# A second expert bias in TensorE's sums: a two-part F32R product in place of two VectorE operations per tile

## What is computed

```python
x = x + gnn(layernorm(x), adj, ...)              # 32 graphs, hidden width 512
xin = layernorm(x)                               # input of the experts
xn = layernorm_affine(xin, gamma, beta)
logits = xn @ Wr + br                            # 8 experts
top_vals, top_idx = jax.lax.top_k(logits, 2)
w = jax.nn.softmax(top_vals)                     # weights of the two chosen experts
for e in range(8):
    h = gelu(xn @ W1[e] + b1[e])                 # 128 -> 256
    y_e = h @ W2[e] + b2[e]                      # 256 -> 128
    y = y + y_e * w_full[..., e, None]
x = x + y
```

## Time and profile before

| | us |
|---|---|
| median of 3 runs | 456.43 (456.37 to 456.51) |
| the profiled execution | 457.52 |
| its span, first to last instruction | 455.7 |
| TensorE matmul busy | 405.1 |
| TensorE weight load busy | 346.2 |
| VectorE busy | 306.7 |
| ScalarE busy | 278.8 |
| GpSimd busy | 247.0 |

### The profile page before, as it was taken

The page is one execution under the profiler, slowest core; times in us unless marked ns, Lnnn a source line. Parts: engine busy times, 40 slices in busy tenths (PEclk is TensorE's granted clock), DMA queues, the critical chain, the costliest instruction groups (busy, mean ns, idle before and its releaser), DMA issues.

```text
span 455.7 us, 11870 instructions
## 1 busy us (share of the span) xinstructions
PE 405.1 (89%) x2894; PEld 346.2 (76%) x2894; DVE 306.7 (67%) x1303; ACT 278.8 (61%) x645; POOL 247.0 (54%) x315
## 2 busy tenths in 40 slices
PE   0999999999999999999856675999899999999994
PEld 0457777767777777786746675998899899999994
DVE  4487677898887788867745374676566666655562
ACT  1167777777677778777737262666566666534451
POOL 1023347766667876775744536454555655555554
PEclk9999999999999999999996978899999999999998
DMA  6659762333323231011154224455544454333211
GB/s 190 198 169 353 267 195 98 102 108 93 118 79 109 84 117 39 35 49 39 48 156 121 70 63 127 114 151 138 141 136 132 109 139 115 101 104 108 84 36 36
DMA packets 40889, 53.24 MB, mean 117 GB/s; under 512 B 5811, under 2 KB 35635, under 8 KB 40182
## 3 DMA queue, kind: packets, MB, share of 16 engines
q1 hardware_dynamic: 33040, 32.95, 25.9%
q0 software_dynamic: 6096, 18.52, 11.9%
q10 hardware_dynamic: 1686, 1.01, 0.8%
HBM read 37.75 MB, written 22.31 MB: 132 GB/s over the span
## 4 chain that ended last, share of the span: by engine, by line
PE 57%; issue 10%; DVE 10%; DVEq 8%; another core or an unknown queue 5%; ACT 4%; POOL 2%; DMA 2%; ACTq 1%; POOLq 0%
PE banks L576 10%; PE banks L599 10%; PE banks L724 9%; PE banks L737 8%; PE banks L564 6%; PE banks L585 5%; PE banks L621 3%; DVEq L1434 2%; DVEq L1417 2%; PE banks L611 2%; DMA rms_bc<-rms_w 2%; DVE result L1442 2%; PE banks L706 1%; DVEq L1442 1%
## 5 line engine op out<-in xcount | busy, mean ns | idle before, releaser
L526 POOL DMA_INDIRECT out<-result,rows_in x92 | 89.5, 973 | 83.7 <-DVE result L1442 71.8
L737 PE MATMUL banks<-w_sb,hidden_e 128*128 (+1 forms) x736 | 102.2, 283 | 5.9 <-DVE result L1442 5.0
L737 PEld LDWEIGHTS banks<-w_sb,hidden_e 128*128 128x128 f32 x736 | 92.4, 196 | 9.5 <-issue 8.7
L877 ACT ACTIVATE hidden_e<-banks 128x512 f32<-128x512 f32 x92 | 54.9, 597 | 60.9 <-PE banks L724 35.8
L489 POOL DMA_INDIRECT rows_dram<-rows_out,row_of x64 | 66.5, 1039 | 24.8 <-issue 22.0
L599 PE MATMUL banks<-gw_sb,hidden_t 128*128 128x128 f32 x512 | 68.8, 277 | 0.0
L576 PE MATMUL banks<-gw_sb,agg 128*128 128x512 f32 x128 | 67.2, 611 | 0.8 <-ACT agg L812 0.8
L1428 DVE SCALAR_TENSOR_TENSOR acc<-banks,rows_in,acc 128x128 f32<-128x128 f32 x92 | 32.2, 350 | 48.8 <-PE banks L737 21.0
L599 PEld LDWEIGHTS banks<-gw_sb,hidden_t 128*128 128x128 f32 x512 | 63.5, 192 | 0.8
L797 ACT ACTIVATE hidden<-hidden,rrms 128x512 f32<-128x512 f32 x64 | 45.6, 714 | 18.1 <-POOL rrms L466 18.1
L990 DVE TENSOR_TENSOR hidden<-banks,rms_bc 128x512 f32<-128x512 f32 x64 | 43.8, 686 | 13.8 <-ACT hidden L789 13.8
(11 more groups left out here) (141 smaller groups left out, 707.9 us busy)
## 6 DMA issues: line engine op xcount, KB each, us to landing
rows_in<-rows_dram SPq DMA_DIRECT2D x92, 132.5 KB
adj<-adj_t SPq DMA_DIRECT2D x16, 512.0 KB, 3.7
x_tok<-x SPq DMA_DIRECT2D x16, 256.0 KB, 3.7
rows_dram<-idle_in POOLq DMA_DIRECT2D x1, 3710.0 KB
rows_dram<-idle_in SPq DMA_DIRECT2D x28, 132.5 KB
out<-result,rows_in POOLq DMA_INDIRECT x92
w_sb<-w SPq DMA_DIRECT2D x1, 1024.0 KB, 6.3
b_bc<-b SPq DMA_DIRECT2D x1, 1024.0 KB, 11.5
```

The costliest lines, as they stand in the source:

```text
L526: nc.gpsimd.indirect_dma_start(out=out, out_offset=bass.IndirectOffsetOnAxis(ap=rows_in[:, i % RING][:, IDX_AT:IDX_AT + 1].bitcast(U32), a ...
L737: last = pe.matmul(y_ps(i)[:, w], hidden_e[:, i % 4, w * HCE + c], w2_sb[:, bass.ds(at + c * D, D)], start=(c == 0), stop=(c == HCE - 1))
L877: nc.scalar.activation(hidden_e[:, i % 4], h_ps(i), ACT.Gelu).then_inc(gelu_done, 1)
```

## The change

The bias is no longer added by VectorE. For each of a tile's two experts TensorE begins the sum in PSUM with `bias_sel` times the expert's 128 columns of `b2_parts`, an F32R matmul, and the two matmuls of the second layer add to it. `b2_parts` (128 x 1024, zero but for row 0, the rounded bias, and row 32, the remainder) is made once on VectorE in steps 11 to 14, each of its four operations last in its step; the rounded copy in row 32 lies in `b1_bc`. L1417 and L1434 and their waits and semaphores are gone; the low product (L1428 before) now adds the residual values directly. TensorE waits for `b2_split` before its first tile.

```diff
+        b2_parts = sb("b2_parts", [P, E * D], F32R)
+        b2_high = b1_bc[:, 0:E * D].bitcast(F32R)
...
                     for w in range(2):
+                        bias_at = expert(words, i, D, w == 0)
+                        pe.matmul(y_ps(i)[:, w], bias_sel[:], b2_parts[:, bass.ds(bias_at, D)], start=True, stop=False)
                         at = expert(words, i, HE, w == 0)
                         for c in range(HCE):
                             last = pe.matmul(y_ps(i)[:, w], hidden_e[:, i % 4, w * HCE + c],
-                                             w2_sb[:, bass.ds(at + c * D, D)], start=(c == 0), stop=(c == HCE - 1))
+                                             w2_sb[:, bass.ds(at + c * D, D)], start=False, stop=(c == HCE - 1))
...
             pe.wait_ge(table_ready, 2)
+            pe.wait_ge(b2_split, 4)
...
+            def split_b2(k):
+                if k == 0:
+                    dve.wait_ge(folded, FOLDS)
+                    nc.vector.memset(b2_parts[:].bitcast(F32), 0.0).then_inc(b2_split, 1)
+                elif k == 1:
+                    dve.wait_ge(b2_split, 1)
+                    nc.vector.tensor_copy(b2_parts[0:1], b2_bc[0:1]).then_inc(b2_split, 1)
+                elif k == 2:
+                    nc.vector.tensor_copy(b2_high[32:33], b2_bc[32:33]).then_inc(b2_split, 1)
+                else:
+                    dve.wait_ge(b2_split, 3)
+                    nc.vector.tensor_tensor(b2_parts[32:33], b2_bc[32:33], b2_high[32:33].bitcast(F32), ALU.subtract
+                                            ).then_inc(b2_split, 1)
...
+                if s - FOLD_AT - FOLDS in range(4):
+                    split_b2(s - FOLD_AT - FOLDS)
...
             def tile_step(step):
-                if (i := tile_at(step, 0)) is not None:
-                    rows = rows_in[:, i % RING]
-                    if i < NT and i % PER_WORD == 0:
-                        words[i // PER_WORD % 2] = dve.value_load(word[0:1, i // PER_WORD:i // PER_WORD + 1],
-                                                                  min_val=0, max_val=2 ** 24 - 1)
-                    dve.wait_ge(rows_here[i % RING], 16 * (i // RING + 1))
-                    if i >= AHEAD:
-                        dve.wait_ge(result_ready, i - AHEAD + 1)
-                    nc.vector.scalar_tensor_tensor(acc[:, i % AHEAD], b2_bc[:, bass.ds(expert(words, i, D, True), D)],
-                                                   rows[:, bass.ds(expert(words, i, 1, True) + W_AT, 1)],
-                                                   rows[:, X2_AT:X2_AT + D], ALU.mult, ALU.add).then_inc(based, 1)
                 tail(step, 0)
...
-                    dve.wait_ge(base_done, j + 1)
                     dve.wait_ge(y_done, j + 1)
+                    if j >= AHEAD:
+                        dve.wait_ge(result_ready, j - AHEAD + 1)
                     nc.vector.scalar_tensor_tensor(acc[:, j % AHEAD], y_ps(j)[:, 0],
                                                    done[:, bass.ds(expert(done_words, j, 1, True) + W_AT, 1)],
-                                                   acc[:, j % AHEAD], ALU.mult, ALU.add).then_inc(low_added, 1)
+                                                   done[:, X2_AT:X2_AT + D], ALU.mult, ALU.add).then_inc(low_added, 1)
                 tail(step, 1)
-                if i is not None:
-                    dve.wait_ge(based, i + 1)
-                    nc.vector.scalar_tensor_tensor(acc[:, i % AHEAD], b2_bc[:, bass.ds(expert(words, i, D, False), D)],
-                                                   rows[:, bass.ds(expert(words, i, 1, False) + W_AT, 1)],
-                                                   acc[:, i % AHEAD], ALU.mult, ALU.add).then_inc(base_done, 1)
```

More of the change, by code:

```diff
@@ L277, in build @@
         folded = sem("folded")
+        b2_split = sem("b2_split")
         rank_consts = sem("rank_consts")
@@ L337, in build @@
         y_done = sem("y_done")
-        based = sem("based")
-        base_done = sem("base_done")
         low_added = sem("low_added")
@@ L1404, in tail @@
                     table_words(1, 2)
-            words = {}
             def tile_step(step):
-                if (i := tile_at(step, 0)) is not None:
-                    rows = rows_in[:, i % RING]
-                    if i < NT and i % PER_WORD == 0:
-                        words[i // PER_WORD % 2] = dve.value_load(word[0:1, i // PER_WORD:i // PER_WORD + 1],
-                                                                  min_val=0, max_val=2 ** 24 - 1)
-                    dve.wait_ge(rows_here[i % RING], 16 * (i // RING + 1))
-                    if i >= AHEAD:
-                        dve.wait_ge(result_ready, i - AHEAD + 1)
-                    nc.vector.scalar_tensor_tensor(acc[:, i % AHEAD], b2_bc[:, bass.ds(expert(words, i, D, True), D)],
-                                                   rows[:, bass.ds(expert(words, i, 1, True) + W_AT, 1)],
-                                                   rows[:, X2_AT:X2_AT + D], ALU.mult, ALU.add).then_inc(based, 1)
                 tail(step, 0)
```

## The result

The changed kernel takes 460.63 us (median of 5, 458.92 to 461.15) beside 456.43 (5 runs, 456.01 to 457.94): ratio 1.008, 95% interval 1.0053 to 1.0106. So it is 4.2 us slower, where the prediction said 8.4. The profiled execution has a span of 459.35 us against 455.73.

The account below looks back on a forecast made before the run. The prediction took TensorE as the bound (busy 89%), except in the middle expert tiles, where VectorE's 2.13 us per tile set the pace. Its terms summed to +8.4 us on 456.43, giving 464.8 us, range 457.5 to 472.

Parts of the forecast that it names:

- middle: Expert tiles 23 to 62: VectorE's relief and TensorE's price cancel, plus 1 us for remaining waits; +0.9 us.
- end: Expert tiles 63 to 90: TensorE is the whole chain and pays for every bias matmul; +6.3 us.
- head: Expert tiles 0 to 22: about 28 of 44 bias matmuls on the path, against VectorE's relief; +0.7 us.
- split and first bias matmul's start: Splitting b2 on VectorE in steps 11 to 14: 4.0 us of work, mostly covered by TensorE; +0.3 us.
- drain: After the end stretch: last second-layer groups grow while GpSimd's sends set the pace; +0.2 us.
- p = 0.1115: Price in us of one bias matmul in TensorE's stream, taken from fp32 passes with such a load; two per tile.
- Rivals 1: TensorE's bias weight load is hidden under the running pass, 0.05 us per bias matmul: 454.6 us; chance 0.11.
- 3 (p = 0.22): Short F32R bias matmul on TensorE costs two slots like an fp32 one: 482.5 us; chance 0.06.
- allowance of 1 us for TensorE's waits: Tiles 23 to 62: 1 us added for waits that stay, as TensorE's address work grows by two bias offsets per tile.
- Rival 2: Tiles 23 to 62: TensorE's bank waits stay and longer address work makes new holes: 469.2 us; chance 0.15.
- The first step: Start of tiles 0 to 22: last residual and statistics no longer behind removed VectorE operations; 1.5 to 2 us removed.
- rival 4: A hole in tiles 0 to 22 goes or shrinks as GpSimd's sends come earlier, 5.65 us less: 459.2 us; chance 0.08.

Follow-up runs that it names:

- e6: Changed kernel with one 256-column F32R matmul for both biases in the 28 leftover tiles, instead of two of 128: 457.69 us, ratio 1.0023.
- e1: Changed kernel without its 184 bias matmuls, the second bias left out of the result: 444.45 us, ratio 0.9744.
- e2: Kernel before plus the split and the bias matmuls, VectorE's two bias operations kept: 470.22 us, ratio 1.0293.
- e4: Changed kernel with TensorE adding only the low expert's bias in the 64 run-time tiles, VectorE all other biases: 457.87 us, ratio 1.0066.
- e12: Kernel before, unmodified, run again for its profile on a chip with the holes: 456.37 us (one run).
- e11: Changed kernel, unmodified, run again beside the kernel before on a chip with the holes: 460.55 us, ratio 1.0094.
- e17: Changed kernel, unmodified, run once more on a fourth chip with the holes: 459.55 us, ratio 1.0047.
- e5: Changed kernel with the bias of tiles 0 to 22 given back to VectorE: 462.35 us, ratio 1.0151.
- e8: Changed kernel with leftover tiles' biases back on VectorE and 14 GpSimd copies between the head's sends, on the fifth chip: 441.67 us, ratio 1.0051.
- e9: Kernel before with 14 GpSimd copies between the head's sends, on the fifth chip: 442.44 us, ratio 1.0056.
- e10: Changed kernel with 14 GpSimd copies, all of a row's ahead of its first send, on the fifth chip: 448.51 us, ratio 1.0187.
- hybrid: Changed kernel with the 28 leftover tiles' biases given back to VectorE: 454.42 us, ratio 0.9956; repeated on another chip 454.6 us, ratio 0.9971.
- e15: Changed kernel with leftover tiles' biases back on VectorE and 14 GpSimd copies between the head's sends, on a chip with holes: 454.39 us, ratio 0.9915.

## Why the prediction was right in its direction and twice too large

By its own steps, profiled executions, predicted and measured:

| term | predicted | measured |
|---|---|---|
| middle | +0.9 | -0.6 |
| end | +6.3 | +5.8 |
| head | +0.7 | -3.1 |
| split and first bias matmul's start | +0.3 | 0 in the steps; +0.9 in the start |
| drain | +0.2 | +0.6 |
| sum | +8.4 | +3.6 (median +4.2) |

**The price was right.** p = 0.1115 from the earlier trace rows holds: a tile that only TensorE paces went from 1.896 to 2.119 us, two times 0.1115. The end's 28 tiles grew by 5.77 us, 0.103 for each of 56, since small waits of 0.5 us that stood in the end before are gone. Rivals 1 (p = 0.05) and 3 (p = 0.22) fall by the chain rows at 400 us. e6 shows that 256 columns take nearly the same slot. The Trainium skill ("TensorE: Matmul & The Clock Gate", Back-to-back issue gap) gives 81 ns for a stream of load and 128-column matmul pairs; this chain, at 0.1115 us, doesn't agree with it.

**The middle** cancelled as said (e1: -9.1; bias matmuls: +8.5 for 80). The picture behind it was not quite right: "VectorE's 2.13 us per tile hides TensorE's 1.89" holds in 14 tiles of 40 only, the other 26 being TensorE's own, which is why e2 and e4 came out otherwise than expected. The allowance of 1 us for TensorE's waits was wrong: TensorE has no idle time there (84.80 busy of 84.80 us). That its address work then runs ahead is argued, not shown. Rival 2 didn't come, and e4 shows its wait in four tiles.

**The split** cost nothing: the graph layer's 16 steps take 192.6 us with and without it. The 0.9 us lie within the scatter of the start.

**The step that failed is the head.** The prediction wrote: "Removed there: some 1.5 to 2 us. In the routing steps VectorE also has less per step, 0.5 us more. Term: +0.7". The first step gave 2.1 us, as worked out, in every pair of profiles on a chip with holes. What was mis-sized is the rest of the head. The prediction had +2.6 us for it (price 3.1, relief 0.5). Measured, it was -1.0 in the first pair of profiles, 0.0 in the pair on one chip (e12, e11), and +1.1 to +2.0 with e17 against these two profiles of the kernel before. By e1, the relief was 4.85 us in all, not 2.4, and the price 1.8 (67.10 less 65.33), not 3.1, that is some 16 of the 44 bias matmuls on the path instead of 28. e5 gives the other half: with VectorE's operations back in the head it is 69.99 us. So VectorE's shorter work was worth far more in the routing steps than the 0.5 us put in for it; by e1 it was 2.8 (4.85 less the first step's 2.1).

Two things of the head that the prediction didn't weigh, or weighed low, go with this. Neither is separated by a run.

- The holes. This was rival 4, given 0.08. VectorE sets when GpSimd's rows of sends begin (252.36 before, 250.74 after), and the hole ends some 1.5 us after such a row, so the argument "what a hole ends on isn't VectorE by the profile" doesn't exclude VectorE. But how much the holes shrank isn't firm. At the first row one piece of 6.92 us became two, 1.57 and 5.39, the same in sum; at the second 2.52 and 5.65 became 2.95. On one chip (e12, e11) the sums are 10.6 and 9.9, while the head is 2.1 us shorter. And without any hole the head with TensorE's bias is still the shorter one, by 3.6 us (e8, e9).
- The clock. The granted clock is 0.83 in the heads of 69.2 to 70.2 us of the two kernels and 0.87 in those of 67.1 and 67.2. At the lower level (1.2 GHz) eight second-layer records take 1.72 us instead of 0.89. The chain of waits of the kernel before, 254 to 300 us, has both:

```profile
269.58 0.89 PE banks L737 x8
...
287.07 1.72 PE banks L737 x8
```

The size of this term isn't fixed: the changed kernel's head was 67.10, 67.23 and 69.18 in three executions, and the kernel before's 70.18 and 69.29. So the total of 4.2 us, half of what was forecast, is in part luck of the chip and the execution.

**Still open.** Why signals of TensorE seem to reach ScalarE and VectorE late in the holes: the trace has no releaser, and no run here removed the indirect DMAs. TensorE's own last two matmuls in the hole of 255.29 stand apart too (258.53 and 259.24, weight loads waiting on "issue" for up to 1.21 us), so late issue on several engines at once is a rival that nothing here tests. Why one chip hasn't got them. The pages differ in one more thing: part 6 gives the loads of the tiles' rows (`rows_in<-rows_dram`) 2.2 us to landing in the three kernels of the fifth chip and no time in any other. So outside that chip the traces lack the ends of these DMAs, and what waits for one can't be told from them. The changed kernel itself was never run on the fifth chip, so that it is slower there by its whole price (e10's ratio 1.0187 includes the copies) is argued, not shown; so is that the plain hybrid is no slower there.

## What to carry to other kernels

Moving work from an engine with slack to the one that bounds costs its full slot wherever the bound is already full. A mean time per tile hides who sets the pace: look at successive tiles, since the price is paid in each tile that the receiving engine already paces. Put the work only where the relief is worth more: here the run-time tiles pay for it and the 28 leftover tiles don't, and the hybrid is 0.3 to 0.4% under the kernel before (the second of its two intervals just takes in no difference) where the full change is 0.5 to 0.9% over it. Price a small matmul by the slot of the nearest chain rows with the same load, not by its columns. And treat chain pieces of unknown releaser as movable: they can shrink, move, or be absent on another chip, so they belong into the range with more than a small chance.

## What was not expected of the hardware

- On four chips the kernel before took 455.3 to 457.5 us, on a fifth 439.95 (16 runs within 2.6 us): 3.6% for the same program. The heads of three kernels there were 55.5 to 59.2 us, against 63 to 74 elsewhere; middle and end of the same kernels agree to 2 us.
- On the others, ScalarE started 4 us after the end at 256.7 us of the matmul that it waits for (changed kernel), and 8 us after one at 267.5 (e15), while GpSimd sent rows of indirect DMAs. On the fifth chip five sends at 1.27 us distance delayed nothing, where the same five go with a hole of 3.2 to 5.65 us on all others.
- Copies of 0.41 us on GpSimd between those sends, pure extra work, took 3.0 us off the kernel before on one chip (ratio 0.993) and added 2.5 us on the fifth.
- A 256-column F32R matmul with its own weight load takes a slot of 0.12 us in a stream of fp32 matmuls, one of 128 columns 0.11.
